# Cross attention in a decoder layer: three of four turned banks of a step copied by ScalarE, one by VectorE

## What is computed

```python
q, k, v = split_heads(x @ Wq), split_heads(x @ Wk), split_heads(x @ Wv)   # 32 heads of 16, q and k with RoPE
w = softmax(q @ k.T / 4 + attention_mask)                                # 256 x 256 for each head
attn = w @ v
a_k, a_v = split_heads(adapter @ Wk), split_heads(adapter @ Wv)          # adapter: the context, 256 rows of width 512
a_w = tanh(gate) * softmax(q @ a_k.T / 4)
attn = attn + a_w @ a_v
x = layernorm(x + attn @ Wo)
```

## Time and profile before

| | us |
|---|---|
| median of three runs | 2846.16 |
| the profiled execution, device time | 2846.07 |
| its span, first to last instruction | 2844.3 |
| PE busy | 2714.4 (95%) |
| VectorE (DVE) busy | 1863.5 (66%) |
| ScalarE (ACT) busy | 1288.8 (45%) |
| GpSimd (POOL) busy | 475.9 (17%) |
| copies of turned banks on ScalarE, L1252 | 256, mean 0.596 each |
| copies of turned banks on VectorE, L1422 | 256, mean 0.689 each |

### The profile page before, as it was taken

The page is one execution under the profiler, slowest core; times in us unless marked ns, Lnnn a source line. Parts: engine busy times, 40 slices in busy tenths (PEclk is TensorE's granted clock), DMA queues, the critical chain, the costliest instruction groups (busy, mean ns, idle before and its releaser), DMA issues. The chain is left out here.

```text
span 2844.3 us, 80636 instructions
## 1 busy us (share of the span) xinstructions
PE 2714.4 (95%) x34134; PEld 1681.2 (59%) x34134; DVE 1863.5 (66%) x5175; ACT 1288.8 (45%) x3137; POOL 475.9 (17%) x626
## 2 busy tenths in 40 slices
PE   7999999999999999999999889999999999976998
PEld 3565555656555565555556556666666666653466
DVE  5565655656556565665656537888888988886633
ACT  3343333334334343343334226676766767763231
POOL 1111111111111111111111131122131221200020
PEclk9999999999999999999999889999999999998999
DMA  5010110100101101101101100000000000001341
GB/s 190 20 44 5 31 46 20 34 26 21 43 17 32 35 14 31 35 13 31 46 4 30 61 31 1 13 9 6 13 2 13 13 2 13 2 2 69 138 185 67
DMA packets 96774, 99.95 MB, mean 35 GB/s; under 512 B 38176, under 2 KB 84384, under 8 KB 95264
## 3 DMA queue, kind: packets, MB, share of 16 engines
q1 hardware_dynamic: 96256, 94.27, 10.3%
q0 software_dynamic: 160, 0.52, 0.0%
HBM read 89.93 MB, written 4.85 MB: 33 GB/s over the span
## 5 line engine op out<-in xcount | busy, mean ns | idle before, releaser
L200 PE MATMUL dr_p<-x_t,dr_w_g 128*128 128x512 f32 x1536 | 746.8, 613 | 11.1 <-DMA dr_w_g<-in_w_in 7.7
L1246 ACT ACTIVATE xa_probs<-xa_probs,xa_low 128x256 f32<-128x256 f32 x1024 | 430.2, 497 | 17.9 <-DVE xa_low L1413 13.3
L200 PEld LDWEIGHTS dr_p<-x_t,dr_w_g 128*128 128x128 f32 x1536 | 267.1, 192 | 229.2 <-issue 219.3
L1178 PEld LDWEIGHTS xa_t<-ident,xa_probs 128*128 128x128 f32 x2048 | 224.3, 141 | 159.2 <-ACT xa_probs L1246 97.9
L1178 PE MATMUL xa_t<-ident,xa_probs 128*128 128x128 f32 x2048 | 285.5, 280 | 21.8 <-ACT xa_probs_t L1252 15.5
L624 DVE SCALAR_TENSOR_TENSOR dr_acc<-dr_p,dr_taps,dr_acc 128x510 f32<-128x510 f32 (+2 forms) x384 | 285.1, 743 | 24.3 <-ACT dr_acc L487 16.3
L1413 DVE CUSTOM_DVE_ANT_0 xa_probs<-xa_s,xa_mask 128x256 f32<-128x256 f32 x512 | 209.7, 410 | 77.7 <-PE xa_s L1165 77.4
L1252 ACT ACTIVATE xa_probs_t<-xa_t 128x512 f32<-128x512 f32 x256 | 152.6, 596 | 229.8 <-PE xa_t L1178 229.7
L1413 DVE CUSTOM_DVE_ANT_0 xa_probs<-xa_s,xa_zeros 128x256 f32<-128x256 f32 x512 | 214.9, 420 | 0.1
L1422 DVE COPY xa_probs_t<-xa_t 128x512 f32<-128x512 f32 x256 | 176.4, 689 | 41.0 <-PE xa_t L1178 29.8
L487 ACT ACTIVATE dr_acc<-dr_p,dr_taps 128x512 f32<-128x512 f32 x128 | 87.5, 683 | 236.0 <-PE dr_p L200 236.0
(11 more groups left out here) (302 smaller groups left out, 4645.1 us busy)
## 6 DMA issues: line engine op xcount, KB each, us to landing
dr_alpha<-alpha_rows SPq DMA_DIRECT2D x64, 254.0 KB, 4.1
dr_w_g<-in_w_in SPq DMA_DIRECT2D x48, 256.0 KB, 5.9
dr_alpha<-alpha_rows SPq DMA_DIRECT2D x32, 256.0 KB, 5.4
ff_wide<-in_fw_qkv SPq DMA_DIRECT2D x8, 1024.0 KB, 15.4
x_t<-in_x_t SPq DMA_DIRECT2D x4, 1024.0 KB, 7.3
tokens<-in_x_tok SPq DMA_DIRECT2D x1, 4096.0 KB, 16.3
dr_wo_g<-in_w_out SPq DMA_DIRECT2D x8, 512.0 KB, 3.8
xa_ctx_b<-in_ctx_t SPq DMA_DIRECT2D x8, 512.0 KB, 3.9
```

Source lines behind the costliest of these rows:

```text
L200: mm = pe.matmul(bank[:, :], w_g[:, k, m, :], x_t[:, k, 2 * S * batch:2 * S * (batch + 1)], start=(k == 0), stop=(k == KC - 1))
L1178: mm = pe.transpose(bank_t[i % 2][:, at:at + P], probs[:, v % 3, i, kind, kt * P:(kt + 1) * P], ident)
L1246: op = act.activation(at, at, ACT.Exp, bias=low[:, v % 3, i, kind:kind + 1], scale=-1.0)
```

## The change

ScalarE now copies heads 0, 1 and 2, VectorE only head 3. On ScalarE the copy of head 1 stands right behind that of head 0, ahead of the piece taken; on VectorE `copy(u, 0)` is gone. The two counters of copies become three: `copied` for heads 0 and 2, `copied_first` for head 1, `copied_second` for head 3. PE waits accordingly, and the first matmul of `weigh` waits on three counters where it waited on two.

```diff
-        copied = [sem(f"copied{j}") for j in range(2)]
+        copied, copied_first, copied_second = sem("copied"), sem("copied_first"), sem("copied_second")
...
                     wait(pe, exped, 4 * v + i + 1)
-                    wait(pe, copied[i % 2], 2 * v + i // 2)
+                    if i % 2 == 0:
+                        wait(pe, copied, 2 * v + i // 2)
+                    elif i == 1:
+                        wait(pe, copied_second, v)
+                    else:
+                        wait(pe, copied_first, v + 1)
...
             def weigh(v):
-                wait(pe, copied[0], 2 * (v + 1))
-                wait(pe, copied[1], 2 * (v + 1))
+                wait(pe, copied, 2 * (v + 1))
+                wait(pe, copied_first, v + 1)
+                wait(pe, copied_second, v + 1)
...
                 act.activation(probs_t[:, v % 2, 2 * m].rearrange("p k t n -> p (k t n)"), bank_t[0][:, :], ACT.Copy)\
-                    .then_inc(copied[0], 1)
+                    .then_inc(copied, 1)
+                if m == 0:
+                    wait(act, turned[1], 2 * v + 1)
+                    act.activation(probs_t[:, v % 2, 1].rearrange("p k t n -> p (k t n)"), bank_t[1][:, :], ACT.Copy)\
+                        .then_inc(copied_first, 1)
...
-            def copy(v, m):
-                wait(dve, turned[1], 2 * v + m + 1)
+            def copy(v):
+                wait(dve, turned[1], 2 * v + 2)
                 wait(dve, weighed, 4 * (v - 1))
-                dve.tensor_copy(probs_t[:, v % 2, 2 * m + 1].rearrange("p k t n -> p (k t n)"), bank_t[1][:, :]).then_inc(copied[1], 1)
+                dve.tensor_copy(probs_t[:, v % 2, 3].rearrange("p k t n -> p (k t n)"), bank_t[1][:, :]).then_inc(copied_second, 1)
...
                     tops(u + 1, 0)
-                copy(u, 0)
                 if u and u % 2 == 0:
                     turn_mixed(dve, u // 2 - 1)
...
                     tops(u + 1, 1)
-                copy(u, 1)
+                copy(u)
```

## The result

The kernel with the change took 2829.86 us (median of six runs, 2827.52 to 2833.45). The kernel before, run beside it, took 2843.97 us (six runs, 2842.46 to 2847.46). The ratio is 0.9948, with an interval of 0.9938 to 0.9958: 14.1 us faster, and by the interval between 12 and 18. It is 7.6 us under the forecast: 2.2 of these are the median of the kernel before, which had been 2846.16 over three runs, and the other 5.5 are gain that was not forecast.

The account below looks back on a forecast made before the run. PE was taken to bound the cross attention, with 36 us of its idle time to win. Gains of 3.05 + 1.15 + 0.43 + 0.61 + 3.3 = 8.5 us gave 2837.5 us, with an 8-in-10 range of 2834.0 to 2843.0.

Parts of the forecast that it names:

- terms 2, 4 and 5 of the sum: Last batch gains: 1.15 us in steps 114, 116 and 124; 0.61 in step 112; 3.3 over steps 120 to 122.
- what can be won is the 36 us in which PE stands still: Cross attention: PE is busy 851.75 of 888 us, so only its 36 us of idle time can be gained.
- Zero, then: Plain steps: bank 3 is turned about t0+1.95 as before, so moving bank 1's copy gains nothing there.
- Five times 0.61: Choosing steps 32, 48, 64, 80, 96: the idle wait before bank 3's turn goes whole, 3.05 us together.
- The 0.38 of even steps: Uncovered steps where VectorE turns the mixed bank: VectorE's own delay before the weighing, 0.38 us a step, goes.
- Only the waits go: Rival: waits vanish but the low-clock losses stay, gaining 6.4 us, 2839.7 us; chance 0.20.
- all three clock losses go: Rival: the clock losses vanish, step 112's too, gaining 10.1 us, 2836.0 us; chance 0.10.
- Slower, by the clock: Rival: the low clock catches the whole last batch, costing 19.8 us less the 8.5 gained, 2857.4 us; chance 0.06.
- low clock only after step 112: Sign expected in the trace after the change: PE's clock falls behind step 112 and nowhere else.
- Gains before the last batch do not arrive: Rival: steps after choosing steps wait for exponentials, so the 3.05 us is lost, 2840.5 us; chance 0.07.
- eaten: Rival: the weighing's third counter or a ScalarE copy pair without overlap takes 4 to 6 us back, 2842 us; chance 0.10.
- nothing: Rival: copy 3, last of the step, sets everything and VectorE fills freed time with waiting, 2846 us; chance 0.05.

Follow-up runs that it names:

- e4: The change with one counter for all three ScalarE copies, so the weighing waits on two counters: 2827.76 us, ratio 0.9940.
- e3: The kernel before with bank 1's copy moved to ScalarE only in steps 112 to 127: 2837.34 us, ratio 0.9970.
- e8: The change with VectorE's choosing cut in two, rank and choice moved to the end of the next step: 2828.9 us, ratio 0.9943.
- e1: The change plus an unread 128x512 multiply on VectorE where its copy of bank 1 stood: 2836.04 us, ratio 0.9966.
- e2: The kernel before with bank 1's copy moved to ScalarE only in choosing steps 32 to 96 and count steps 40 to 104: 2838.88 us, ratio 0.9972.
- e9: The kernel before with VectorE turning the mixed bank ahead of its copy of bank 1 in even steps: 2857.78 us, ratio 1.0040.
- e10: The change with choosing cut in two, and bank 3 on ScalarE in steps 6, 7, 112 to 117, 123 to 125: 2824.45 us, ratio 0.9926.

## Why the prediction was right in kind and too small

- **The mechanism held where the prediction looked.** The waits on VectorE before a turn vanished, the copy of bank 1 in step 124 ran within 0.02 us of the forecast, the third counter cost nothing (e4), 120 kept its clock and ScalarE's table load became the limit of 121 (1.13 us idle before its turns). Step 122 was put at 6.8 us at full clock; e3 and e8, which kept it there, have 6.76. The last batch gained 5.13 us to step 125; terms 2, 4 and 5 of the sum made 5.06. That they agree so closely is luck: 0.44 in step 113, 0.13 in 112 and 0.05 in each plain step were not in the sum, and steps 120 to 122 fell 1 us short of it, since 122 ran at the low clock. The 0.44 in step 113 is mostly clock: the earlier trace rows stop at its start, and the low clock that they show went on.
- **The step that failed is "what can be won is the 36 us in which PE stands still".** From it followed a sum made only of idle marks, with every step that shows none on VectorE, or that has a projection, at nothing. But PE's busy time fell too, by 9.6 us, some 1.6 of it by estimate clock: PE also waits inside its groups, and this is counted as busy. The five count steps, which the sum does not name, gave 2.64 us: VectorE's count and maxima held up PE's weight loads there. They have no projection between the turns either, so that clause does not cover them. The evidence stood in the trace of before: a score group of 1.41 us, where the earlier trace rows have 1.14 unhindered. The chain of waits and the idle marks do not show it, and these alone were read. e1 shows that VectorE's time gives this gain, since with the filler nothing of it is left, and e2 that it comes in these steps by themselves.
- **"Zero, then" for a plain step was 0.05 us.** Bank 1 is seen 0.05 earlier from ScalarE than from VectorE; the text had the sign and bounded it at 0.03, for 44 waits. With one step in each batch going the other way by 0.05 it gave 1.29 us before the last batch and some 0.5 in it. Why step 3 of a batch is longer was not tried.
- **Five times 0.61 was five times 0.74.** The row is of step 48, not 64, by the count of turns; the five steps are alike. There the second half of the eight turns started 1.22 us after the first (2042.86 and 2044.08), where unhindered starts are 0.44 apart: 0.78 us of delay, of which the mark shows 0.62, since a lone group's modelled end lies 0.16 behind its next possible start. The scores took 0.07 back. The same holds for step 7: 0.57 for a mark of 0.43. Together 0.8 us. The text also took the whole wait as gone because ScalarE is free, and the copy of bank 3 as hidden; e1 shows that the second needs VectorE's 0.6 us, without which 0.13 us is left.
- **The 0.38 of even steps was right in size and wrong in reason.** The text called it VectorE's delay by the mixed bank; e1 and e9 show it to be the mixed bank's delay by a copy that waits.
- **The rivals.** "Only the waits go" was right about the clock at 112 and 122 of this execution, and wrong about 120 and about the total; "all three clock losses go" happened in e3's trace and not in this one. "Slower, by the clock" did not come: 5.76 us in all plain steps, and no low clock in new places. The sign "low clock only after step 112" failed at 122, where it was low before too. Both outcomes occur at 112 and 122 for the same work there (e3). "Gains before the last batch do not arrive" was refuted by e2, "eaten" by e4 and by ScalarE's pitch of 0.49 us, "nothing" by the total. No rival stood for more gain than 10.1 us, and the range was too narrow for that reason: each term was costed from its idle mark, with nothing held open for waiting that has none.

## What to carry to other kernels

Before costing a relief of an engine, compare the lengths of like groups and the distances of their starts over all steps, not only the idle marks: a score group of 1.41 us beside others of 1.14 is a wait. List every consumer of the late engine's results, small ones too (here the seat copy and the next maxima). And an instruction that stands waiting on its engine delays whatever is written behind it: moving it to an engine that is idle at that moment gains this delay even where the first engine is kept as busy (e1, 0.38 us a step), whereas moving it back on its own engine (e9) can cost more than it saves.

## What the runs showed of the hardware

- The same instructions, with 2.68 or 2.69 us of PE idle before them, ran once at a granted clock of 0.54 (the change) and once at 1.00 (e3); with 1.24 or 1.25 us, at 0.57 and 1.00 (step 122 of the same two). A fall costs 1.2 to 1.4 us. That such falls make part of the spread between executions is likely from the mean clocks of the six runs, but only one execution of each kernel has a trace. With 0.73 (e10) or 1.48 us (e8) idle at step 112 the clock stayed full in the one execution seen of each.
- Copies of 128x512 fp32 out of a bank take 0.591 to 0.597 us on ScalarE and 0.689 on VectorE, and the next instruction starts 0.49 us behind the first on ScalarE.
- A third counter in the waits of a matmul costs less than 0.02 us a step (e4).
